# The first 24 row tiles of each expert stage run while the last token group is still routed

## What is computed

```python
x = x + attn_a(layernorm(x))      # causal attention over 512 keys, 16 heads of 8
x = x + ffn(layernorm(x))
x = x + attn_b(layernorm(x))      # per token: its 16 heads attend to each other
x = x + ffn(layernorm(x))

def ffn(x):                       # 24 experts, each token goes to 2
    topk_val, topk_idx = top_k(x @ gate_w + gate_b, 2)
    gates = softmax(topk_val)
    y_e = gelu(x @ w1[e] + b1[e]) @ w2[e] + b2[e]      # 128 -> 512 -> 128
    return sum_k gates_k * y_{idx_k} + x
```

## Time and profile before

| | us |
|---|---|
| median of 3 runs | 1136.45 (1131.69 to 1137.49) |
| the profiled execution, its own time | 1134.0 |
| its span in the trace | 1132.3 |
| PE busy | 984.7 (87%) |
| DVE busy | 771.3 (68%) |
| ACT busy | 697.0 (62%) |
| POOL busy | 730.7 (65%) |

### The profile page before, as it was taken

The page is one execution under the profiler, slowest core; times in us unless marked ns, Lnnn a source line. Parts: engine busy times, 40 slices in busy tenths (PEclk is TensorE's granted clock), DMA queues, the critical chain, the costliest instruction groups (busy, mean ns, idle before and its releaser), DMA issues.

```text
span 1132.3 us, 28694 instructions
## 1 busy us (share of the span) xinstructions
PE 984.7 (87%) x9446; PEld 773.4 (68%) x9446; DVE 771.3 (68%) x2181; ACT 697.0 (62%) x2115; POOL 730.7 (65%) x1065
## 2 busy tenths in 40 slices
PE   4999999999999952999999799999989736999995
PEld 2555555555555532999999477777777626999995
DVE  3687888888788843445555688899898872445543
ACT  3578787777878731555556467667666433565553
POOL 8655467768567324566766777698898463666664
PEclk8699999999999985999999899899999867999998
DMA  9999981000000004777774899990000016777873
GB/s 338 406 405 405 376 268 66 14 11 19 9 14 21 14 15 118 207 210 231 219 222 137 343 406 408 407 336 21 16 17 13 20 43 182 209 209 236 255 233 95
DMA packets 121864, 203.13 MB, mean 179 GB/s; under 512 B 13296, under 2 KB 67240, under 8 KB 121590
## 3 DMA queue, kind: packets, MB, share of 16 engines
q1 hardware_dynamic: 111462, 184.08, 48.3%
q0 software_dynamic: 9728, 16.95, 4.5%
q10 hardware_dynamic: 528, 0.26, 0.1%
HBM read 76.72 MB, written 127.65 MB: 180 GB/s over the span
## 4 chain that ended last, share of the span: by engine, by line
PE 40%; POOL 21%; issue 16%; DVE 15%; ACT 6%; DMA 1%; POOLq 1%; SPq 0%; DVEq 0%; ACTq 0%
POOL rows_out L893 15%; PE bank L1121 8%; PE bank L1508 6%; PE bank L1469 5%; POOL SETTLE L892 3%; PE bank L1429 3%; DVE NMP L1688 3%; PE bank L1450 2%; PE bank L1424 2%; PE bank L1487 2%; ACT bank L1180 2%; DVE QK L1223 1%; POOL rows_in L700 1%; PE bank L1101 1%; DVE PT L1234 1%
## 5 line engine op out<-in xcount | busy, mean ns | idle before, releaser
L921 ACT ACTIVATE QT<-bank,B 128x128 f32<-128x128 f32 x704 | 201.1, 368 | 181.0 <-PE bank L943 180.9
L1630 ACT ACTIVATE PT<-bank 128x512 f32<-128x512 f32 x320 | 188.2, 604 | 68.3 <-PE bank L1450 68.0
L893 POOL DMA_INDIRECT rows_out<-Y,XI x176 | 174.9, 994 | 84.1 <-POOL SETTLE L892 79.1
L943 PE MATMUL bank<-XIT,PT 128*128 128x128 f32 x1408 | 191.9, 281 | 0.8 <-DVE XIT L1002 0.7
L954 PE MATMUL bank<-W,QT 128*128 x1408 | 187.3, 276 | 1.3 <-ACT QT L921 1.3
L1058 POOL TENSOR_TENSOR PT<-PT 128x512 f32<-128x512 f32 x128 | 158.3, 1266 | 40.5 <-ACT PT L1164 40.4
L943 PEld LDWEIGHTS bank<-XIT,PT 128*128 128x128 f32 x1408 | 174.4, 195 | 2.8 <-DVE XIT L1002 1.7
L954 PEld LDWEIGHTS bank<-W,QT 128*128 128x128 f32 x1408 | 172.2, 193 | 1.6 <-issue 1.6
L700 POOL DMA_INDIRECT rows_in<-XG,POS x128 | 126.5, 988 | 49.4 <-issue 33.4
L1469 PE MATMUL bank<-KT,QT 48*128 48x384 bf16 (+3 forms) x512 | 122.2, 310 | 10.5 <-DVE NMP L1684 8.6
L1007 DVE TENSOR_TENSOR YB<-bank,B2R 128x128 f32<-128x128 f32 x176 | 51.3, 292 | 116.7 <-PE bank L954 116.4
(11 more groups left out here) (220 smaller groups left out, 2023.1 us busy)
## 6 DMA issues: line engine op xcount, KB each, us to landing
rows_in<-XI SPq DMA_DIRECT2D x32, 3120.0 KB, 30.8
PT<-in_w_dram SPq DMA_DIRECT2D x176, 256.0 KB
XI<-rows_in SPq DMA_DIRECT2D x176, 65.0 KB
PT<-rows_out SPq DMA_DIRECT2D x31, 256.0 KB, 3.9
W<-in_w2pack_dram SPq DMA_DIRECT2D x4, 1536.0 KB, 14.4
rows_in<-XI SPq DMA_DIRECT2D x2, 1560.0 KB, 30.6
rows_out<-Y,XI POOLq DMA_INDIRECT x176
X<-in_h_dram SPq DMA_DIRECT2D x8, 256.0 KB, 5.3
```

The source lines that it names most:

```text
L893: pool.indirect_dma_start(out=rows_out, out_offset=bass.IndirectOffsetOnAxis(ap=XI_I[:, u, D + 1:D + 2], axis=0), in_=Y[:, u % 4, :], in_o ...
L921: a = act.activation(HT[:, u % 2, c, :], psH[u % 2][:, c * P:(c + 1) * P], ACT.Gelu, bias=B1[:, bass.ds(e * FC + c, 1)])
L943: mm = pe.matmul(psH[u % 2][:, c * P:(c + 1) * P], W1[:, u, c * P:(c + 1) * P], XIT[:, u % 2, :], start=True, stop=True)
L1630: act.activation(PT[:, m % PT_SLOTS, :], psB[m % 2][:, :], ACT.Exp, scale=float(D) ** -0.5).then_inc(exp_done, 1)
```

## The change

**What runs when.** The first `EARLY` = 24 row tiles of a stage take only whole 128-row tiles out of groups 0 to 5; their tables come from an early count after group 5 (`early_step`, 21 steps with 22 instructions, during attention: slots n = 303 to 309 of attention A, tiles T = 32 and 33 of attention B). The other 64 tiles' tables are made later from what the early ones left. The number of tiles stays 88. Groups are fetched and combined a few tiles later than before.

**What moves into the first tiles of the expert stage** (`last_group_pe`, `_act`, `_dve`, `_pool`): the routing of group 7; the 16 table instructions over seven groups and the 13 of the last; the eight sends of group 6, one ahead of each of the settling operations of tiles 0 to 7; the eight sends of group 7, in tiles 12 to 16; in stage 0 the two `route_keep`s of groups 6 and 7, in tiles 4 and 22. The exponential of group 7's gates becomes a power of e on GpSimd, at tile 7. SyncE waits for the second tables ahead of tile 24 and for the sends of all groups ahead of its rows. The result's second PSUM buffer becomes bank 6 instead of 5.

```diff
+EARLY_GROUPS = GROUPS - 2
+EARLY = STEP * (-(-(2 * EARLY_GROUPS * GT * P - NE * (P - 1)) // P) // STEP)
+EARLY_CELLS = EARLY_GROUPS * NE
+EARLY_SLOT, EARLY_SLICE = 345, 4 * GROUPS + 5
...
+FETCH_AT = [last_tile_of(g) + STEP + 2 * g * (g < 3) for g in range(GROUPS - 1)]
+COMBINE_AT = [last_tile_of(0) + 6]
+for g in range(1, GROUPS - 1):
+    COMBINE_AT.append(max(last_tile_of(g) + 6, COMBINE_AT[-1] + (8 if g < 3 else 4)))
+SEND_AT = [min(at + 12, ROW_TILES - 1) if g < GROUPS - 2 else ROW_TILES for g, at in enumerate(COMBINE_AT)]
...
+            for n in range((TPB - AHEAD) * STEPS, EARLY_SLOT):
...
             pe.wait_ge(r_xg, n + 1)
             wait(pe, r_pos, n)
+            if n == EARLY_GROUPS:
...
+        def route_power_of_e(pool, n):
+            pool.wait_ge(r_top, n + 1)
+            pool.tensor_tensor(EXPD[:, :], EULER[:, :], TDIF[:, :], ALU.pow).then_inc(r_exp, 1)
...
+        def early_step(dve, ph, i):
...
+        def turned_tables(ph, late):
+            bank, at = (banks[0], 0) if (ph, late) == (1, 0) else (psG, 0)
+            return [bank[0:1, at + i * P:at + i * P + (ROW_TILES - EARLY if late else EARLY)] for i in range(2)]
...
+        def last_group_pe(pe, ph, j):
+            n = GROUPS * (ph + 1) - 1
+            if j == 0:
+                route_transpose(pe, n, 1)
+            if j == 2:
+                route_logits(pe, n)
+            if j == 9:
+                route_ranks(pe, n)
+            if j == 17:
+                turn_tables(pe, ph, 1)
+        def last_group_act(act, ph, j):
+            n = GROUPS * (ph + 1) - 1
+            if j == 0:
+                route_copy(act, n)
+            if j == 1:
+                route_second(act, n, 1)
+            if ph == 1 and 2 <= j < 2 + GT:
+                keep_scaled(act, n, TILES - GT, (j - 2,))
+        def last_group_dve(dve, ph, j):
+            n = GROUPS * (ph + 1) - 1
+            for i in ((0, 1, 2), (3, 4, 5), (6, 7), (8,), (9,), (10,), (11,), (12,), (13, 14, 15))[j] if j < 9 else ():
+                head_step(dve, ph, i)
+            if 2 <= j < 8:
+                route_top(dve, n, 2 * (j - 2))
+                route_top(dve, n, 2 * (j - 2) + 1)
+            for i in {9: (0,), 10: (1,), 11: (2, 3)}.get(j, ()):
+                route_rows(dve, n, 1, i)
+            if 12 <= j < 16:
+                for i in range(3 * (j - 12), 3 * (j - 12) + 3):
+                    tail_step(dve, ph, i)
+            if j == 17:
+                whole_tables(dve, ph, 1)
+        LAST_SENDS = {12: ((0, 0), (0, 1)), 13: ((1, 0),), 14: ((1, 1), (2, 0)), 15: ((2, 1),), 16: ((3, 0), (3, 1))}
+        def last_group_pool(pool, ph, j):
+            n = GROUPS * (ph + 1) - 1
+            if j < 2 * GT:
+                route_send(pool, n - 1, 0, ((j // 2, j % 2),))
+            if j == 7:
+                route_power_of_e(pool, n)
+            if ph == 0 and j == 4:
+                route_keep(pool, GROUPS - 2, 0, GT * (GROUPS - 2))
+            if j == 12:
+                route_settle(pool, n)
+            if j in LAST_SENDS:
+                route_send(pool, n, 1, LAST_SENDS[j])
+            if ph == 0 and j == 22:
+                route_keep(pool, GROUPS - 1, 1, GT * (GROUPS - 1))
...
             def read(c):
+                if c == EARLY // STEP:
+                    eng.wait_ge(e_tables, 2 * ph + 2)
                 if c < ROW_TILES // STEP:
                     now[c % 2] = [r(STEP * c) for r in readers[c % 2]]
...
-            sp.wait_ge(e_tables, ph + 1)
+            sp.wait_ge(e_tables, 2 * ph + 1)
+            if ph == 0:
+                sp.wait_ge(pv_done, UNITS - 1)
+            else:
+                sp.wait_ge(b_prod, 4 * TILES)
...
+                if j in (0, EARLY):
+                    for i in range(j, j + WEIGHTS_AHEAD):
+                        ask_for_weights(i)
+                if j + WEIGHTS_AHEAD < EARLY or EARLY <= j < ROW_TILES - WEIGHTS_AHEAD:
+                    ask_for_weights(j + WEIGHTS_AHEAD)
                 sent_before(sp, ph, j, STEP)
                 if j == 0:
                     emptied(sp, ph, GROUPS // 2 - 1)
+                if j in (0, EARLY):
                     for par in range(2):
-                        sp.wait_ge(r_scat[par], 16 * GT * GROUPS * (ph + 1))
+                        groups = GROUPS // 2 * ph + (EARLY_GROUPS if j == 0 else GROUPS) // 2
+                        sp.wait_ge(r_scat[par], 16 * 2 * GT * groups)
                 load_rows(j, u)
+            def ask_for_weights(j):
+                if j >= STEP:
+                    sp.wait_ge(f_up, base + j - STEP + 1)
+                load_weights(j, j % STEP)
...
             def body(j, u):
+                last_group_pool(pool, ph, j)
                 pool.wait_ge(f_y, base + j + 1)
                 wait(pool, e_settled, base + j)
                 pool.tensor_tensor(SETTLE[:, 0:1], ONE[:, :], ONE[:, :], ALU.mult).then_inc(e_settled, 1)
...
+            if ph == 0:
+                for t in range(GT):
+                    route_normalize(act, GROUPS - 1, 1, TILES - GT, t)
+            act.wait_ge(e_tables, 2 * ph + 1)
             act.wait_ge(w2_in, 16 * (NE // W2_EXPERTS + 1))
...
             def body(j, u):
+                last_group_pe(pe, ph, j)
                 if j + 1 < ROW_TILES:
                     up(j + 1, (u + 1) % STEP)
                 if j + 2 < ROW_TILES:
                     turn(j + 2, (u + 2) % STEP)
                 down(j, u)
-            pe.wait_ge(e_flat, ph + 1)
-            for i in range(2):
-                mm = pe.matmul(psG[0:1, i * P:i * P + ROW_TILES], ERF[:, i:i + 1], IDF[0:ROW_TILES, 0:ROW_TILES],
-                               start=True, stop=True)
-            mm.then_inc(e_turned, 1)
-            pe.wait_ge(e_tables, ph + 1)
+            if ph == 0:
+                pe.wait_ge(max_done, STEPS * UNITS)
+            pe.wait_ge(e_tables, 2 * ph + 1)
             pe.wait_ge(w2_in, 16 * (NE // W2_EXPERTS + 1))
             turn(0, 0)
             turn(1, 1)
             up(0, 0)
...
                     xi_copy(j + 2, (u + 2) % STEP)
                 gated(j, u)
+                last_group_dve(dve, ph, j)
                 for g in range(GROUPS - 1):
-                    step = j - combine_at(g)
+                    step = j - COMBINE_AT[g]
...
+            over_rows(body, read_ahead(dve, ph, f"dve_expert{ph}", (EJ, NE - 1)))
+            for g in range(GROUPS):
+                for step in range(4):
+                    if g == GROUPS - 1 or COMBINE_AT[g] + step >= ROW_TILES:
+                        combine(dve, ph, g, step)
...
-            for T in range(-3, TILES + 3 * GT):
+            for T in range(-3, EARLY_SLICE):
...
-                if s % GT == 1 and routed(g - 3) and g >= GROUPS:
-                    rows = [(t, k) for t in range(GT) for k in range(2)]
-                    route_send(pool, GROUPS + g - 3, (g - 3) % 2, rows)
-                if s % GT > 0 and routed(g - 3) and g < GROUPS:
+                if s % GT > 0 and routed(g - 3):
                     rows = (((0, 0), (0, 1), (1, 0)), ((1, 1), (2, 0), (2, 1)), ((3, 0), (3, 1)))[s % GT - 1]
                     route_send(pool, GROUPS + g - 3, (g - 3) % 2, rows)
...
                     route_logits(pe, GROUPS + g - 2)
+                if T == EARLY_SLICE - 3:
+                    turn_tables(pe, 1, 0)
...
+                if T == EARLY_SLICE - 5:
+                    for i in range(11):
+                        early_step(dve, 1, i)
+                if T == EARLY_SLICE - 4:
+                    for i in range(11, 21):
+                        early_step(dve, 1, i)
+                if T == EARLY_SLICE - 2:
+                    whole_tables(dve, 1, 0)
...
-            for u in range(TPB - AHEAD - 1, UNITS + 10):
+            for u in range(TPB - AHEAD - 1, UNITS + 3):
...
-            route_keep(pool, GROUPS - 1, (GROUPS - 1) % 2, GT * (GROUPS - 1))
+            route_deviation(pool, GROUPS - 1)
+            route_numbers(pool, GROUPS - 1, 1, TILES - GT)
+            route_settle(pool, GROUPS - 2)
             experts_pool(pool, 0)
             attb_pool(pool)
             experts_pool(pool, 1)
...
+                    if g == EARLY_GROUPS - 1 and j == 51:
+                        turn_tables(pe, 0, 0)
...
-                    if g == GROUPS - 2 and j == 43:
-                        dve.wait_ge(scoresB_done, STEPS * UNITS)
-                        head_tables(dve, 0)
+                    if g == EARLY_GROUPS - 1 and 43 <= j < 50:
+                        for i in range(3 * (j - 43), 3 * (j - 43) + 3):
+                            early_step(dve, 0, i)
+                    if g == EARLY_GROUPS - 1 and j == 53:
+                        whole_tables(dve, 0, 0)
...
-            expert_tables(dve, 0)
+            dve.wait_ge(x1_done, BATCH)
+            for i in range(6):
+                route_stats(dve, GROUPS - 1, TILES - GT, i)
             experts_dve(dve, 0)
             attb_dve(dve)
-            expert_tables(dve, 1)
```

267 lines of the change are left out of this document (171 added, 96 removed).

## The result

The changed kernel takes **1115.9 us** (median of 4 runs, 1115.24 to 1119.12) against 1134.07 for the kernel before (the three runs of the start and one more, 1128.33 to 1137.49): ratio 0.985, 95% interval 0.9801 to 0.990. The forecast was 1111 in a range of 1099 to 1125. The profiled execution took 1115.77 us, its span is 1114.0; against the 1134.0 us of the profiled execution before it gained 18.2 us, where the sum had 25.

The account below looks back on a forecast made before the run. It took two TensorE holes ahead of the expert stages, then GpSimd's scatters, as the bound. Gains of 14.4 and 11.4, together 25.8, less 1 for slow products, gave 25: 1111 us on the median's scale, range 1099 to 1125.

Parts of the forecast that it names:

- Tile 0 in stage 0: First result's scatter in the first expert stage, claimed at 429.4 in place of 454.17, 24.8 us earlier.
- The early steps: 22 new VectorE instructions in attention A's slots 303 to 309, summed to 6.8 us, taken as 6.0 of delay.
- Tile 0 in stage 1: First result's scatter in the second expert stage, claimed at 932.2, 20.4 us earlier, with the rows as the limit.
- Tiles 0 to 16: GpSimd's scatters, sends and extra work over these tiles, claimed at 44.4 us in stage 0, 43.0 in stage 1.
- Sends beside VectorE cost nothing: All 16 sends a stage beside VectorE's two-port operations, claimed to cost nothing by the median row of 959 ns.
- Rivals 1 and 4: GpSimd stays at slow spacing, 6.4 us a stage, chance 0.12; VectorE's work holds sends, 4.5 a stage, chance 0.05.
- rival 5: TensorE's clock falls while it idles through 17 tiles and stays low beyond, making the kernel slower, 1173; chance 0.05.
- Rival 2: The stage's start costs less: early steps half recovered, TensorE warm after tile 16, sends overlap settling; 1100, chance 0.12.
- rival 6: Early tables or rows come late, so the stage starts with the old wait; 1136, chance 0.02.
- Tile 22, 8.3 behind tile 16: Scatter-to-scatter distance across tile 24's row load: landing 2.4, issue and load 3.0, products 1.3, scatter 1.6 us.
- Stage lengths: Tile 0's scatter to tile 87's, claimed at 179.7 us in stage 0 and 178.3 in stage 1.
- Rival 3: At tile 24 the pipeline empties and TensorE pays load and restart, 6.0 us a stage, 1123; chance 0.10.

Follow-up runs that it names:

- the second trace: The changed kernel, unedited, profiled again in a later session beside two other kernels; 1116.62 us, ratio 0.9844 to the kernel before.

## Why the prediction was nearly right, step by step

- **Tile 0 in stage 0, 24.8 us earlier: right.** From the copy near 306 us it is 148.57 - 123.91 = 24.66. The early steps were put at 6.0 and cost 6.04 to the last unit's copy (94.90 us from the mark against 88.86) and 6.14 by taking them away. But the 6.0 stood for table steps on VectorE alone, and these cost 4.7; the other 1.4 came through TensorE's clock, which the prediction did not have here, and in two of eight traces only 0 or 0.7 did. That the two make 6 is luck. The idle 3.4 us of the earlier trace rows were no cushion.
- **Tile 0 in stage 1, 20.4 earlier: right.** 53.07 - 32.62 = 20.45; the second trace gives 19.8. In the profiled pair only 17.6 show (329.1 against 311.5 from one stage to the next), because attention B took 2.8 us more in that execution; the second trace of the changed kernel has 275.78, as before. Of the 2.8, 2.2 are in its first slice, 17.9 us at a granted clock of 0.85 against 15.7 at 0.98. The chain was the forecast one: statistics late, power, last sends, landing, rows. In it two small errors cancel: the last send started 17.6 us behind the mark in attention B and not 18.5, and from it to the scatter were 15.1 us and not 14.3.
- **Tiles 0 to 16, 44.4 and 43.0: right.** They took 43.64 and 43.14. The spacing was 2.66 with a send and 1.39 without, where I had 2.69 and 1.43.
- **Sends beside VectorE cost nothing: right** (median 963 ns). The rows named for it did not show that, since before no send stood beside a result's scaling; the 13 sends of the changed kernel that do are the evidence. Rivals 1 and 4 fall with these two; rival 5 too: the clock was 1.00 and 0.96 through tiles 0 to 16 of the two stages, with TensorE busy for 40.35 of 43.64 us. Rival 2 falls with the 6.04 and the dry seam, rival 6 with the start.
- **Tile 22, 8.3 behind tile 16: wrong.** It was 10.7 and 9.5 (484.82, 977.17), and 10.5 and 10.9 in the second trace. The failed step is "SyncE can ask for tile 24's rows when tile 16's scatter has landed, 2.4, and issue and load take 3.0": the request went out at 3.2, behind four weight loads that I left out of SyncE's queue at that place, though the scatter had landed after 2.3, and TensorE had the rows 3.7 after it. Then tile 22 took 3.8 and not 2.9, after a wait and with the clock at 0.76 from 479 to 486 us. In stage 1 the landing itself came last, 3.55 in place of 2.4, beside the same burst of loads; the request went out at 3.7 and the rows were there 2.9 later. With this, TensorE's lead of four tiles, on which the sum counted for giving back 3.1 us of the stage's delay, is used up at the seam: tiles 16 to 24 took 14.9 and 13.7 us against 15.4 and 15.6 before, 0.5 and 2.0 given back.
- **Stage lengths** therefore were 182.6 and 178.9, not 179.7 and 178.3, and 181.3 and 180.9 in the second trace, so the sum had 3.4 and 4.2 too little over the two stages of either trace. Tiles 22 to 87, put at 127.0, took 128.3 and 126.2.
- The sum: 24.7 + 17.6 gained, 13.2 + 9.8 given up, 19.2; attention A was already 1.0 us later at the mark: 18.2. Of the 7.6 us between 25.8 and 18.2, attention B took 2.8, the mark 1.0, and the stage lengths 3.4; the seam alone has 3.6, and the other terms of the stages cancel. The last 0.4 is small change, 0.2 of it stage 1 before, which had 169.1 and not 169.3. The 1 us taken off for slow products was about right: at stage 0's seam two groups of eight took 1.91 and 1.51 in place of 1.06 each, 1.3 in all, and at stage 1's hardly any. The seam and attention B are why the gain is 18 and not 25; the seam repeats in the second trace, attention B doesn't.

Rival 3, that a dry seam costs 6.0 a stage, was there in part: the seam did run dry, and cost 1.2 to 2.5 us a stage over the 8.3.
